# One store per head pair and four loads per double step, in place of four stores and one load per pair, for the transposed softmax probabilities of a fused attention block

## The reference

```python
h = _ln(x, g1, be1)
x = _attn(h, h, Wq1, Wk1, Wv1, Wo1, bo1) + x
h = _ln(x, g2, be2)
x = _attn(h, context, Wq2, Wk2, Wv2, Wo2, bo2) + x
h = _ln(x, g3, be3)
a, gate = (y[..., :FF_HID], y[..., FF_HID:])          # y = h @ Wp + bp
x = a * jax.nn.gelu(gate, approximate=False) @ W2 + b2 + x
```

## Time and profile before

| | |
|---|---|
| Time, median of 3 runs | 2994.09 us (2993.19 to 2994.99) |
| Profiled execution: its own time | 2995.35 us |
| its span, first to last instruction | 2993.6 us |
| TensorE busy | 2937.4 us, 98% of the span |
| VectorE, ScalarE, GpSimd busy | 74%, 62%, 48% |
| Packets of the main DMA queue | 70.5% of 16 DMA engines' span |
| DMA to and from DRAM | 640.80 MB in 475245 packets |

### The profile page before, as it was taken

One profiled execution on the slowest core, in us unless ns is written; L12 is line 12 of the kernel. 1 busy time (PEld: TensorE's weight loads), 2 busy tenths in 40 slices (PEclk: granted clock), 3 DMA queues, 4 the chain that ended last, 5 costly groups with the idle time before them and its releaser, 6 DMA issues. The chain is left out here.

```text
span 2993.6 us, 75871 instructions
## 1 busy us (share of the span) xinstructions
PE 2937.4 (98%) x25480; PEld 2572.7 (86%) x25480; DVE 2229.3 (74%) x3314; ACT 1855.6 (62%) x5622; POOL 1450.5 (48%) x1012
## 2 busy tenths in 40 slices
PE   7999999999999999999999999999999979999999
PEld 6888888888888888888888888888888868888888
DVE  5777777777777777778888888888878756566664
ACT  6666666666666666767777777777777733332322
POOL 4555555555555555656556566665566531111110
PEclk9999999999999999999999999999999989999999
DMA  8887888788888888888888888888888841112211
GB/s 238 238 243 244 244 244 245 242 244 245 243 244 244 243 245 241 272 253 262 260 255 259 257 259 259 257 258 260 257 258 257 252 138 56 56 63 66 67 56 36
DMA packets 475245, 640.80 MB, mean 214 GB/s; under 512 B 58945, under 2 KB 405953, under 8 KB 474945
## 3 DMA queue, kind: packets, MB, share of 16 engines
q1 hardware_dynamic: 473824, 639.96, 70.5%
q10 hardware_dynamic: 1376, 0.27, 0.1%
HBM read 338.57 MB, written 301.47 MB: 214 GB/s over the span
## 5 line engine op out<-in xcount | busy, mean ns | idle before, releaser
L638 POOL TENSOR_TENSOR at_probs<-at_probs,at_row_inv 128x1024 f32<-128x1024 f32 x512 | 968.4, 1894 | 780.6 <-DVE at_row_inv L834 780.3
L688 ACT ACTIVATE at_probs<-at_ps_s,at_neg_max 128x256 f32<-128x256 f32 x2048 | 943.6, 476 | 169.5 <-DVE at_neg_max L807 153.5
L807 DVE TENSOR_REDUCE at_neg_max<-at_ps_s 128x4 f32<-128x1024 f32 x512 | 624.5, 1220 | 191.7 <-PE at_ps_s L978 188.9
L826 DVE STREAM_TRANSPOSE at_blocks<-at_probs 128x1024 f32<-128x1024 f32 x512 | 631.2, 1233 | 15.2 <-POOL at_probs L638 15.2
L997 PE MATMUL at_ps_o<-at_probs_t,at_v 128*64 128x256 f32 x4096 | 500.9, 386 | 3.5 <-DMA at_probs_t<-at_turns 3.5
L741 ACT ACTIVATE at_qk_hi<-at_ps_qk 128x512 fp32r<-128x512 f32 x512 | 306.3, 598 | 296.1 <-PE at_ps_s L978 183.6
L910 PE MATMUL at_ps_qk<-at_h_hi,w_hi 128*128 128x256 f32 x1536 | 428.7, 302 | 13.5 <-ACT at_h_hi L711 5.4
L688 ACT ACTIVATION_READ_ACCUMULATOR at_probs<-at_ps_s,at_neg_max 128x1 f32 x2048 | 425.3, 208 | 1.2 <-issue 1.2
L997 PEld LDWEIGHTS at_ps_o<-at_probs_t,at_v 128*64 128x64 f32 x4096 | 272.1, 137 | 150.2 <-issue 3.8
L910 PE MATMUL at_ps_qk<-at_h_hi,w_lo 128*128 128x256 f32 x1536 | 397.4, 281 | 0.0
L910 PEld LDWEIGHTS at_ps_qk<-at_h_hi,w_hi 128*128 128x128 f32 x1536 | 289.8, 189 | 119.7 <-issue 104.6
(11 more groups left out here) (110 smaller groups left out, 6647.8 us busy)
## 6 DMA issues: line engine op xcount, KB each, us to landing
at_turns<-at_blocks SPq DMA_DIRECT2D x2048, 128.0 KB, 2.5
at_probs_t<-at_turns SPq DMA_DIRECT2D x512, 512.0 KB, 4.5
at_xt<-in_x SPq DMA_DIRECT2D x32, 256.0 KB, 5.4
at_xres<-in_x SPq DMA_DIRECT2D x32, 256.0 KB, 3.3
after_self_attention<-at_yout SPq DMA_DIRECT2D x32, 256.0 KB, 2.6
at_xt<-after_self_attention SPq DMA_DIRECT2D x32, 256.0 KB, 5.6
at_xres<-after_self_attention SPq DMA_DIRECT2D x32, 256.0 KB, 3.6
after_cross_attention<-at_yout SPq DMA_DIRECT2D x32, 256.0 KB, 2.5
```

The lines of the kernel that those rows point to most:

```text
L638: pool.tensor_tensor(tile, tile, scale, ALU.mult).then_inc(probs_ready, 1)
L688: last = act.activation(probs[:, slot % 2, h, t], scores[:, slot % 2, h, t], ACT.Exp, bias=neg_max[:, slot % 2, i:i + 1], accum_out=row_su ...
L807: nc.vector.tensor_reduce(neg_max[:, slot].rearrange("p (h t) -> p h t", h=2), scores[:, slot], AX_X, ALU.max, negate=True).then_inc(neg_m ...
L826: nc.vector.transpose(blocks[:, slot].rearrange("p (j a q) -> p a j q", j=QUADS, q=QUAD), probs[:, slot].rearrange("p h t (k j q) -> p (h ...
```

## The change

For each pair the four stores of 32 partitions each become one store of 128 partitions. The DRAM tensor `turns` is laid out anew: both pairs of a double step lie side by side in it, so that for one source partition and one target quarter there are 2 KB in one piece (even pair's 1 KB, odd pair's 1 KB). For each double step the two loads (one a pair, 128 partitions with one piece of 4 KB each) become four, one for each quarter of 32 target partitions, with four pieces of 2 KB for each partition. The tile `probs_t` keeps its size, now as two slots of a double step each. The semaphores follow: one `turn_stored` for both pairs, which the loads wait for until both are stored; two `turn_loaded`, one for each double step's slot.

```diff
@@ -445,8 +445,8 @@
         probs = sb("probs", [P, 2, 2, TT, SEQ], F32)
 
         blocks = sb("blocks", [P, 2, QUADS * TURN], F32)
-        probs_t = sb("probs_t", [P, RING, QUADS * TURN], F32)
-        turns = nc.dram_tensor(tag + "turns", [PAIRS, QUADS, QUAD, QUADS, TURN], F32).ap()
+        probs_t = sb("probs_t", [P, 2, QUADS, 2 * TURN], F32)
+        turns = nc.dram_tensor(tag + "turns", [PAIRS // 2, QUADS, QUAD, QUADS, 2, TURN], F32).ap()
         neg_max = sb("neg_max", [P, 2, 2 * TT], F32)
         row_sum = sb("row_sum", [P, RING, 2 * TT], F32)
         row_inv = sb("row_inv", [P, RING, 2 * TT], F32)
@@ -494,8 +494,8 @@
         inv_ready = sem("inv_ready")
         probs_ready = sem("probs_ready")
         turned = sem("turned")
-        turn_stored = [sem("turn_stored0"), sem("turn_stored1")]
-        turn_loaded = [sem(f"turn_loaded{i}") for i in range(RING)]
+        turn_stored = sem("turn_stored")
+        turn_loaded = [sem("turn_loaded0"), sem("turn_loaded1")]
         pv_done = sem("pv_done")
         o_hi_ready = sem("o_hi_ready")
         o_ready = sem("o_ready")
@@ -507,7 +507,7 @@
 
         def stored_count(b, q):
 
-            return 16 * QUADS * (PAIRS // 2 * b + q // 2 + 1)
+            return 32 * (PAIRS // 2 * b + q // 2 + 1)
 
         block = es.enter_context(nc.Block())
 
@@ -540,22 +540,21 @@
                 s = PAIRS * b + p - TURNED
                 slot = (p - TURNED) % PAIRS
                 sp.wait_ge(turned, s + 1)
-                for i in range(QUADS):
-                    sp.dma_start(turns[slot, :, :, i].rearrange("j k n -> k j n"),
-                                 blocks[QUAD * i:QUAD * (i + 1), slot % 2].rearrange("k (j n) -> k j n", j=QUADS)
-                                 ).then_inc(turn_stored[slot % 2], 16)
-
-            def load_turn(b, p):
-
-                slot = (p - LOADED) % PAIRS
-                sp.wait_ge(turn_stored[slot % 2], stored_count(b, p - LOADED))
-                sp.dma_start(probs_t[:, slot % RING], turns[slot].rearrange("j k i n -> (j k) (i n)")
-                             ).then_inc(turn_loaded[slot % RING], 16)
+                sp.dma_start(turns[slot // 2, :, :, :, slot % 2].rearrange("i k j n -> (i k) j n"),
+                             blocks[:, slot % 2].rearrange("p (j n) -> p j n", j=QUADS)).then_inc(turn_stored, 16)
+
+            def load_turns(b, p):
+
+                slot = (p - LOADED) % PAIRS // 2
+                sp.wait_ge(turn_stored, stored_count(b, p - LOADED))
+                for j in range(QUADS):
+                    sp.dma_start(probs_t[QUAD * j:QUAD * (j + 1), slot % 2],
+                                 turns[slot, :, :, j].rearrange("i k s n -> k i (s n)")
+                                 ).then_inc(turn_loaded[slot % 2], 16)
 
             def step(b, p, part, stage):
-                for pair in (p, p + 1):
-                    if alive(part, pair, LOADED):
-                        load_turn(b, pair)
+                if alive(part, p, LOADED):
+                    load_turns(b, p)
                 if ahead(part, stage) and p == 0:
                     load_next(b + 1, stage_ahead(part, stage))
                 for pair in (p, p + 1):
@@ -822,7 +821,7 @@
                 slot = (p - TURNED) % 2
                 dve.wait_ge(probs_ready, s + 1)
                 if counts(c := stored_count(b, p - TURNED - 2)):
-                    dve.wait_ge(turn_stored[slot], c)
+                    dve.wait_ge(turn_stored, c)
                 nc.vector.transpose(blocks[:, slot].rearrange("p (j a q) -> p a j q", j=QUADS, q=QUAD),
                                     probs[:, slot].rearrange("p h t (k j q) -> p (h t k) j q", j=QUADS, q=QUAD)
                                     ).then_inc(turned, 1)
@@ -987,9 +986,10 @@
                 pe.wait_ge(v_ready, PAIRS // 2 * seq + q // 2 + 1)
                 if counts(c := PAIRS // 2 * b + (p - WEIGHTED) // 2):
                     pe.wait_ge(o_ready, c)
-                slot = (p - WEIGHTED) % RING
-                pe.wait_ge(turn_loaded[slot], 16 * (PAIRS // RING * b + (p - WEIGHTED) // RING + 1))
-                turned_t = probs_t[:, slot].rearrange("p (i h t k q) -> p h k t i q", h=2, t=TT, k=TT, q=QUAD)
+                slot = (p - WEIGHTED) // 2 % 2
+                pe.wait_ge(turn_loaded[slot], 16 * QUADS * (PAIRS // RING * b + (p - WEIGHTED) // RING + 1))
+                turned_t = probs_t[:, slot, :, (p - WEIGHTED) % 2 * TURN:((p - WEIGHTED) % 2 + 1) * TURN
+                                   ].rearrange("p i (h t k q) -> p h k t i q", h=2, t=TT, k=TT, q=QUAD)
                 half = q % 2
                 for k in range(TT):
                     for h in range(2):
```

## The result

The changed kernel takes 3116.89 us (median of 4 runs, 3115.5 to 3124.85) against 2993.64 us before (median of 4, so not quite the 2994.09 of the three earlier runs); the ratio is 1.0416, with a 95% interval of 1.0400 to 1.0432. The forecast was no change, with a range up to 3014 us. The profiled execution took 3124.85 us.

A forecast was written before the change was run, and what follows sets the result against it. TensorE was taken as the bound, hiding every edit but 1.5 us at the seam: 2995.35 - 1.5 = 2993.9, less 1.3 for the profiled execution's excess over the median, 2992.6 us. Range 2986 to 3014 us.

The forecast's parts named there:

- What bounds the kernel before: Both attention stages: TensorE sets the time, a double step each 9.28 us; its waits for `probs_t` total 3.5 us.
- Issuing on SP: SP's queue: six DMAs a double step, 4.2 us even at 0.7 us each, against about 4.4 before; no new bound.
- Stores: Stores of a double step: 46 ns a 1 KB piece instead of 61, saving 0.96 us of each DMA engine, at least 0.
- the place of the sum: Cross attention's double step with the next sequence's `x` and context issued before its stores; chain 9.4 us against 11.27.
- Loads: Four 32-partition loads a double step: 3.1 to 4.9 us of each DMA engine, taken as 4.0; 5.5 us to last landing.
- the slow end: 32-partition loads at 215 GB/s: 4.9 us of engine work, 6.4 us from first issue to last landing.
- The shared semaphore: First load also waits for the odd store, already in the chain; VectorE absorbs the first 2.9 us of delay.
- The chain: From the odd turn through store and loads to TensorE: 7.4 us fast, 9.4 middle, 11.1 slow.
- budget of 11.27: Cross attention: us from the odd pair's turn ending at 2041.82 to TensorE taking the even pair at 2053.09.
- Work of the DMA engines: Cross attention, per 9.28 us: 7.9 us now; after, 6.9 fast, 7.8 middle, 8.7 slow, 9.7 if stores save nothing.
- Rival 1: Cross attention: late 32-partition loads, about 0.8 us in each of 32 sequences, 26 us, 3019 us; chance 24%.
- Rival 2: VectorE waits for the shared semaphore, some 0.3 us in 32 to 64 places, about 3008 us; chance 3%.

The follow-up runs named there:

- e8: Kernel before with one store and one load of 128 partitions a pair, 4 KB pieces, own waits, regrouping left out (output differs): 2989.4 us.
- e1: Changed kernel with each of the four loads writing its 2 KB pieces to all 128 partitions, regrouping left out (output differs): 3017.6 us.
- e4: Changed kernel with its four loads issued in the order of quarters 0, 2, 1, 3: 3057.8 us.
- e5: Kernel before with each pair's load cut into two DMAs of 64 partitions, 4 KB pieces, own waits: 3001.8 us.
- e9: e7 with the joint wait put back: SP's loads and VectorE's turns wait for both pairs' stores: 3056.3 us.
- e2: Kernel before with each pair's load cut into four DMAs of 32 partitions, 4 KB pieces, own waits: 3009.7 us.
- e10: e7 with the joint wait for both pairs' stores on SP's loads only, VectorE's turns keeping their own: 3056.5 us.
- e7: Kernel before with one 128-partition store and four 32-partition loads in 1 KB pieces for each pair, each pair waiting for its own store: 2993.5 us.
- e6: Kernel before with loads in four quarters, and loads and VectorE's turns waiting for both pairs' stores: 3242.1 us.

## Why the prediction was wrong

- **What bounds the kernel before** was right: e8 shows that TensorE is the bound and that a faster trip gains 4 us at most.
- **Issuing on SP** was right: the new stores above take 518 to 574 ns to issue, under the 0.7 us that was allowed, in place of four at 440.
- **Stores.** Their landing was the term that was off most: "Store: 2.8 us quiet, 4.7 with the backlog of now [...]; I take 3.9". At the place of the sum the odd store was issued at 2099.4 and landed 6.8 us later; from the end of its turn to the first load it was 6.9 us (2106.25 - 2099.35). The median over all stores is 5.9. Their own cost is not what went wrong: 1 KB packets have a mean of 50 ns in the cross window, 56 before, 46 in the forecast.
- **Loads.** For the time from the first issue to the last landing I took 5.5 us, and 6.4 as the slow end; measured 2113.2 - 2106.25 = 7.0. The work on the DMA engines was off by little: 512 packets of 2 KB at 137 ns on 16 engines are 4.4 us, where I had 4.0 in the middle and 4.9 at the slow end. The rest, 2.6 us, is where I had 1.45 from one quiet load., which I set against the slow end, had stores of all four quarters, so of both halves, in the queue; it was no test of transfers to one half alone, and why it reached 339 GB/s no run shows. The Trainium skill's port rule, which I had set beside the sum, is borne out by e1, e4 and e5 in direction, but not as half rate: 2 KB packets into quarters take 137 ns against 103 into all partitions (e1).
- **The shared semaphore** was the step whose failure decided: "It gains nothing and loses the early start of the even load, which is in the chain above already." e9 puts a price on this wait alone: 63 us. The chain was added up once, from an odd turn to TensorE, with a fixed backlog. But the joint wait closes it to a ring: stores land behind the loads that were issued before them, and all of the next loads wait for those stores. A longer load then makes the store late, and the late store the next load. At the place of the sum the chain became 2113.2 - 2099.35 (the odd turn's end, 2098.10 + 1.25) = 13.9 us against a budget of 11.27, where my sum had 9.4 and its slow end 11.1: 3.0 us of the difference to 9.4 are the store, 1.5 the loads. Before, the even pair's load went out about 1.2 us ahead of the odd one's and so overlapped with the odd store.
- **Work of the DMA engines** against the period was the wrong test. The changed kernel waits at a share of 0.86; e2 and e5 reach 0.93 and 0.95 and lose 16 and 8 us. What tells them apart is the length of the ring.
- **Rivals.** Rival 1 named the place and the cause (late 32-partition loads) but priced it as one lateness of 0.8 us a sequence, 26 us, and let self attention off; TensorE was idle 27 us in the window of self attention alone, and it waited in 156 places, not 32. So the 24% on rival 1 bought the right place, but not the mechanism that set the size. Rival 2, VectorE's wait, shows in the trace (13.1 us in 26 places), but e10 against e9 finds no cost of its own; in the changed kernel itself it was not taken out.

Left open: how the 60 us between e9 and the changed kernel divide. The changed kernel has loads in pieces of 2 KB, stores in 1 KB pieces, and TensorE's wait of the even pair for all four loads; e9 has more DMAs on SP. No run takes these apart. The pieces have a part at least in the DMA engines' work: the packets' time on each engine is 0.674 x 3052.9 = 2058 us in e9 and 2283 in the changed kernel, 0.88 us a double step less, though both load into quarters. Nor was the changed kernel run with nothing but the joint wait taken out; e7 and e9 stand in for that.

## What to carry to other kernels

When a transfer A must land before B is issued, and the next A stands behind B in a queue, they form a ring: add up its whole round, with the landings, and compare that with the period; a sum over one pass, or the share of busy DMA engines, does not show it. Merging two semaphores to save issues removes the overlap that kept the ring short, so try it with each part's own wait first: e7 does the same regrouping in its loads and loses nothing, and e9, the same with the joint wait, loses 63 us. Where loads that write only a part of the partitions are on such a ring, try them alternating between 0 to 63 and 64 to 127; the order alone was worth 59 us here.

## What was unexpected of the hardware

- The order 0, 2, 1, 3 of four loads into quarters of the partitions took 59 us off 3117 (e4), with the same bytes and packets, although the mean 2 KB packet only went from 137 to 132 ns.
- Cutting a 128-partition load in two halves of 64 raised the DMA share in cross attention from 0.85 to 0.95 (e5), more than four quarters did (0.93, e2).
- Two edits that cost 16 and 5 us alone cost 248 us together (e6), with 7.4 us of each round of 9.58 spent on issuing DMAs.
